# A running sum of squared keys moved from VectorE to GpSimd, with earlier weight cuts, moved stores and re-ordered openings

## The chip, the cores and the metric

The kernel runs on one core of one Trainium2 chip, as one launch. The metric is device time in microseconds (us) of that core. Its engines are TensorE (PE in the profile), VectorE (DVE), ScalarE (ACT), GpSimd (POOL) and SyncE (SP), each with its own instruction stream in program order; they wait for each other by semaphores. DMA queues are fed by the engines that issue the transfers.

## The reference, cut to what matters

Two layers follow each other on x (16 x 128 x 512) with a context ctx of the same shape: first an mLSTM attention over a normalised x and a routed feed-forward layer of eight experts, then cross-attention in 16 heads of 128, with an image part and a text part of the keys, and a feed-forward layer with three-valued weights.

```python
x = x + mlstm(layernorm(x), ctx, ctx)
x = x + routed_ffn(layernorm(x))
x = x + cross_attention(layernorm(x), ctx)
x = x + ternary_linear(x)
# in cross_attention, for the image and the text keys:
k = rms_norm(ctx_part @ k_w + k_b, scale)      # mean of squares over all 16 x 128 columns
q = rms_norm(x @ q_w + q_b, scale)
out = softmax(q k^T / sqrt(128)) v             # per head
```

The change is about the mean of squares in `rms_norm` of the keys: the squares of every head's key rows are added up over the heads, so that one row of sums per token comes out.

## The kernel before

All work is one chain of stages on PE's instruction stream: values (0 to about 195 us), heads (195 to 475), the shared feed-forward part (475 to 560), routed experts (560 to 782), queries (782 to 1005), and attention with the last layer (1005 to the end). float32 products are made as three passes of a leading and a trailing part of each factor (`three_passes`, lines 120 to 122); a weight is therefore cut into a lead (ACT) and a trail (DVE) before PE uses it.

In **heads** two things run interleaved. The mLSTM runs in 4 groups g of 4 batches, with 16 slots n per group, one per head. The keys of the later cross-attention are formed in 64 units u, each 12 matmuls of one head's weight with one group's context; `KEYS` lists them, and a unit stands in a slot of `body(g, first)`. In group 0 the 12 units stand in the slots of `OPENING`, from group 1 on the unit of slot n is u = 16 g + n - 4, and four come after the last slot.

- PE: in each slot a key unit, at n % 4 == 2 scores and outputs, at n % 4 == 3 the turn of the heads (line 1311), which needs hT gathered by DVE (line 1147) in the same slot. A key unit u uses one of three banks and so waits for the square of unit u - 3.
- ACT: the lead of the next unit's weight (`weight_lead`, key_lead, line 1387), exponentials for the decay matrix (line 1008), then key and square of the unit of slot n - 1 (`keep_key`, lines 1045 and 1050). The square waits until the sum of unit u - 2 is done.
- DVE: gather, the decayed matrix of the next slot (line 1120), `weight_trail` (key_trail, line 1392), `add_square` (line 1192, the running sum `total`), and small statistics; in slot 14 it waits for `res_done` and takes the statistics of x_kept (line 137).
- POOL: in each slot the causal mask (line 917) of slot n + 5, and from group 1 on, for the group before, `scale` in slots 8 and 9 (line 935, waits for `fac_done`), `weigh` in 10 and 11 (line 945) and `add` in 12 and 13 (line 954, sends `res_done`). `value` (line 925) runs in slots 5 to 7.
- SP: loads of the slots ahead; in slot 10, after loads that wait for scores, the eight loads of the next group's context parts (of_shared_split from ctx_split, line 1382).

A weight is cut at the unit that first uses it (`FIRST_OF`), into the buffer that alternates by unit. In **values**, SP stores the cut context to ctx_split at u = 30, 32, 34 and 36, beside the stores of the transposed x (line 325) for which ACT waits (line 438). In **routed**, the cuts of the tokens for the second tile (`lead_of`, `trail_of`) stand in the first slot. In **queries**, DVE normalises x in four batches per group and signals once per group; PE then transposes (line 2707).

## Time and profile before

| what | value |
|---|---|
| runs | 1359.07, 1366.83, 1367.22 us; median 1366.83 |
| profiled execution | 1370.19 us, span 1368.5 us |
| mean granted clock of PE | 0.976 |
| busy share of the span | PE 95%, DVE 61%, ACT 54%, POOL 28% |
| heads, 195 to 475 us | PE busy 254.81 of 280.00 us, POOL 131.96, DVE 200.94, ACT 200.73 |

The profile is of one execution, and its times are read from the start of the span. A group of the table of lines has its busy time, the mean of one instruction, and the idle time of the engine before its instructions with what ended it. In the timeline, the bracket at the end of a row is the idle time of the engine before it and the instruction that ended it. Instructions of one engine overlap a little, so the distance between two starts can be shorter than the duration of the first.

### The profile page before, as it was taken

Reading aid. Unit: us, or ns where it says so; the run is one execution under the profiler, and the core shown is the slowest. Engines: PE = TensorE matmul, PEld = TensorE weight load, DVE = VectorE, ACT = ScalarE, POOL = GpSimd, SP = SyncE. Lnnn points to the kernel's source line nnn. Section 1 sums busy time; section 2 is a strip of 40 time slices with the busy share of each in tenths; the row PEclk is TensorE's granted clock in tenths of the full one; section 3 lists DMA queues with packets and bytes.
Section 4 is the critical chain, followed back from the end, with each engine's and each line's share of the span. In section 5 each row is a group of like instructions: output and inputs, shape, how many; then the busy total and the mean of one; then the engine's idle time right before and its main releaser. Section 6 shows DMA issues by size and latency. Waiting matters only on the chain. (4 is left out here: it accounts for less than half of the span.)

```text
span 1368.5 us, 24512 instructions
## 1 busy us (share of the span) xinstructions
PE 1298.8 (95%) x7390; PEld 1072.4 (78%) x7391; DVE 840.9 (61%) x1614; ACT 742.9 (54%) x1839; POOL 382.6 (28%) x358
## 2 busy tenths in 40 slices
PE   7998998989999899899989989999989999999998
PEld 6786876767776768688876678888878888888887
DVE  3644546767679774444444377635477777777865
ACT  4334538786777351345455545544676555556651
POOL 0111014273719006399331153036000000000041
PEclk9999999999999899999999999999999999999999
DMA  7847799877787194675648787473565555555403
GB/s 250 307 186 266 265 319 311 267 252 244 258 254 231 63 333 183 204 218 156 201 147 269 265 256 214 137 232 132 185 202 161 162 158 165 159 168 155 122 32 123
DMA packets 168183, 280.99 MB, mean 205 GB/s; under 512 B 29920, under 2 KB 58336, under 8 KB 167840
## 3 DMA queue, kind: packets, MB, share of 16 engines
q1 hardware_dynamic: 142288, 224.44, 51.6%
q0 software_dynamic: 8672, 29.37, 6.6%
q10 hardware_dynamic: 17136, 26.09, 5.2%
q8 instruction: 47, 0.77, 0.2%
q14 instruction: 40, 0.33, 0.1%
HBM read 171.04 MB, written 108.80 MB: 204 GB/s over the span
## 5 line engine op out<-in xcount | busy, mean ns | idle before, releaser
L120 PE MATMUL banks<-of_shared_split,key_lead 128*128 128x512 f32 x256 | 110.0, 430 | 17.5 <-DVE key_trail L1392 10.7
L2973 ACT ACTIVATE prob<-banks,attend_row,rq 128x128 f32<-128x128 f32 x248 | 110.4, 470 | 0.0
L2986 ACT ACTIVATE attend_ol<-banks,of_attend_vbias 128x512 fp32r<-128x512 f32 x64 | 44.2, 691 | 116.9 <-PE banks L3185 116.9
L120 PE MATMUL banks<-wo,attend_ol 128*128 (+1 forms) x256 | 106.3, 415 | 0.0
L121 PE MATMUL banks<-of_shared_split,key_lead 128*128 128x512 f32 x256 | 104.9, 410 | 0.0
L122 PE MATMUL banks<-of_shared_split,key_trail 128*128 128x512 f32 x256 | 104.8, 410 | 0.0
L120 PE MATMUL banks<-queries_rows_split,queries_wl 128*128 128x512 f32 x256 | 100.9, 394 | 0.0
L122 PE MATMUL banks<-wo,attend_ot 128*128 (+1 forms) x256 | 100.8, 394 | 0.0
L121 PE MATMUL banks<-wo,attend_ol 128*128 (+1 forms) x256 | 100.0, 391 | 0.0
L122 PE MATMUL banks<-queries_rows_split,queries_wt 128*128 128x512 f32 x256 | 99.9, 390 | 0.0
L121 PE MATMUL banks<-queries_rows_split,queries_wl 128*128 128x512 f32 x256 | 99.8, 390 | 0.0
L2955 POOL TENSOR_TENSOR x_kept<-x_kept,attend_tern_bias 128x512 f32<-128x512 f32 x12 | 15.5, 1293 | 282.9 <-ACT of_attend_raw L3012 281.0
L2623 DVE TENSOR_TENSOR queries_total<-queries_total,queries_sq 128x512 f32<-128x512 f32 x60 | 45.5, 759 | 74.8 <-ACT queries_sq L2536 74.8
L2532 ACT ACTIVATE queries_head<-banks,queries_bias 128x512 f32<-128x512 f32 x64 | 44.1, 689 | 81.7 <-PE banks L122 76.5
L1008 ACT ACTIVATE heads_dec<-mlstm_gmax,mlstm_nat 128x128 f32<-128x128 f32 x264 | 83.7, 388 | 8.5 <-POOL mlstm_gmax L917 4.8
L120 PE MATMUL banks<-of_shared_split,of_ctx_lead 128*128 128x512 f32 x208 | 84.3, 406 | 1.4 <-DVE of_ctx_trail L479 1.2
L1192 DVE TENSOR_TENSOR heads_total<-heads_total,heads_ksq 128x512 f32<-128x512 f32 x60 | 54.8, 913 | 45.2 <-ACT heads_ksq L1050 45.2
L122 PE MATMUL banks<-of_shared_split,of_ctx_trail 128*128 128x512 f32 x208 | 82.1, 395 | 0.0
L121 PE MATMUL banks<-of_shared_split,of_ctx_lead 128*128 128x512 f32 x208 | 82.0, 394 | 0.0
L3074 DVE TENSOR_TENSOR x_kept<-x_kept,banks 128x512 f32 (+1 forms) x64 | 44.0, 688 | 60.8 <-PE banks L122 60.2
L120 PEld LDWEIGHTS banks<-of_shared_split,key_lead 128*128 128x128 f32 x256 | 51.0, 199 | 35.6 <-DVE key_trail L1392 14.5
L917 POOL TENSOR_SCALAR_AFFINE_SELECT mlstm_gmax<-mlstm_gmax 128x512 f32<-128x512 f32 x69 | 52.6, 777 | 78.6 <-DMA mlstm_gmax<-running_max 78.4
(399 smaller groups left out, 3569.5 us busy)
## 6 DMA issues: line engine op xcount, KB each, us to landing
mlstm_gmax<-running_max SPq DMA_DIRECT2D x36, 512.0 KB, 5.8
k_heads<-heads_key ACTq DMA_DIRECT2D x64, 256.0 KB, 4.5
q_heads<-queries_head SPq DMA_DIRECT2D x64, 256.0 KB, 2.7
q_ahead<-q_heads SPq DMA_DIRECT2D x64, 256.0 KB, 4.2
of_attend_k<-k_heads SPq DMA_DIRECT2D x60, 256.0 KB, 4.0
of_attend_v<-v_heads SPq DMA_DIRECT2D x60, 256.0 KB, 3.3
key_raw<-in_L_xattn_ki_w SPq DMA_DIRECT2D x20, 512.0 KB, 5.4
sorted_rows<-of_shared_split SPq DMA_DIRECT2D x2, 5120.0 KB, 28.6
```

The source lines that it names most:

```text
L120: nc.tensor.matmul(out, lead_l, lead_r, start=first, stop=False)
L121: nc.tensor.matmul(out, lead_l, trail_r, start=False, stop=False)
L122: return nc.tensor.matmul(out, trail_l, lead_r, start=False, stop=last)
L917: nc.gpsimd.affine_select(out=t, in_=t, compare_op=ALU.is_ge, fill=FAR, base=0, pattern=[[0, GB], [1, S]], channel_multiplier=-1).then_inc ...
L1008: ins = nc.scalar.activation(dec[:, n % 2, b], gmax[:, h // 2 % 4, h % 2 * N + b * S:h % 2 * N + (b + 1) * S], ACT.Exp, scale=-1.0, bias=M ...
L1192: nc.vector.tensor_tensor(t, t, ksq[:, m % 2, :], ALU.add).then_inc(total_done, 1)
L2532: nc.scalar.activation(head[:, u % HEADS_RING, :], ps[:, u % 4, :], ACT.Identity, bias=bias[:, h:h + 1]).then_inc(head_done, 1)
L2623: nc.vector.tensor_tensor(t, t, sq[:, u % 2, :], ALU.add).then_inc(total_done, 1)
L2955: nc.gpsimd.tensor_tensor(K.x[:, b, :], K.x[:, b, :], tern_bias[:], ALU.add).then_inc(tern_bias_done, 1)
L2973: ins = nc.scalar.activation(prob[:, j % 2, b, :], ps[:, j % 2, b * S:(b + 1) * S], ACT.Exp, bias=row[:, j % 2, 1, b:b + 1], scale=rq[:, b ...
L2986: nc.scalar.activation(ol[:, par, j, :], ps[:, 4 + j % 2, :], ACT.Identity, bias=vbias[:, bass.ds(quad_of(it) * 4 + j, 1)]).then_inc(ol_do ...
L3074: nc.vector.tensor_tensor(xb, xb, ps[:, 6 + b % 2, :], ALU.add).then_inc(acc_done, 1)
```

## The change

The running sum of squares moves from DVE to POOL, for all units but the last five, which stay on DVE in the tail. In POOL's body it stands behind the mask and ahead of `value`, `scale`, `weigh` and `add`. The order of `KEYS` changes so that in the middle pairs the two units with the same weight stand next to each other; weight buffers alternate by weight; lead and trail of a weight are formed in the slot `SPLIT_AT`, up to one unit ahead of its first use. The split loads of slot 10 come first in that slot. In the tail the last units' operations are re-ordered on ACT and DVE. In values the stores to ctx_split go out at u = 21, 22, 25 and 26, and a load of x one unit later. In routed the cuts of the second tile come before other cuts. In queries the normalised batches are signalled one by one, and for the first group PE transposes batch by batch.

```diff
-        TOKENS = {4: 0, 5: 1, 7: 2, 9: 3}
+        TOKENS = {4: 0, 5: 1, 8: 2, 9: 3}
+        SPLITS = {21: 0, 22: 1, 25: 2, 26: 3}
...
-                if u % 2 == 0 and 30 <= u < 30 + 2 * G:
-                    g = (u - 30) // 2
+                if u in SPLITS:
+                    g = SPLITS[u]
...
-            for k in range(G + 1) for p in range(HALF // 2) for g in (k - 1, k) if 0 <= g < G for j in range(2)]
+            for k in range(G + 1) for p in range(HALF // 2)
+            for g, j in ([(g, j) for g in (k - 1, k) for j in range(2)] if p in (0, HALF // 2 - 1) else
+                         [(g, j) for j in range(2) for g in (k - 1, k)]) if 0 <= g < G]
...
+    SPLIT_AT = [0, 0] + [max(LAST_OF[v - 2] + 2, FIRST_OF[v] - 1) for v in range(2, VISITS)]
+    FORMED = dict((SPLIT_AT[v], v) for v in range(2, VISITS))
...
                 for n in range(PER):
+                    if not first and not last and n == PER - 2 - LAG:
+                        sp.wait_ge(product, CLOSES[g - 1] + 1)
+                        for part in range(2 * C):
+                            A.load_split(sp, g + 1, part)
...
-                    if not first and not last and n == PER - 2 - LAG:
-                        sp.wait_ge(product, CLOSES[g - 1] + 1)
-                        for part in range(2 * C):
-                            A.load_split(sp, g + 1, part)
...
+            def add_square(g, m):
+                u = unit_number(g, m)
+                of = KEYS[u][1]
+                t = total[:, of * N:(of + 1) * N]
+                pool.wait_ge(ksq_done, u + 1)
+                if u == OPENS[of]:
+                    nc.gpsimd.tensor_scalar(t, ksq[:, m % 2, :], 1.0, None, ALU.mult).then_inc(total_done, 1)
+                else:
+                    pool.wait_ge(total_done, u)
+                    nc.gpsimd.tensor_tensor(t, t, ksq[:, m % 2, :], ALU.add).then_inc(total_done, 1)
+
             def body(g, first):
                 for n in range(PER):
                     mask(g, n + AHEAD)
+                    keys_at(g, n, -1, add_square, first)
...
-                if u == FIRST_OF[v] and v >= 2:
+                if u in FORMED:
+                    v = FORMED[u]
                     act.wait_ge(product, LAST_OF[v - 2] + 1)
-                    A.weight_lead(act, KEYS[u][0], v // 4)
+                    A.weight_lead(act, KEYS[FIRST_OF[v]][0], v // 4)
...
                     keys_at(g, n, 1, weight_trail, first)
-                    keys_at(g, n, -1, add_square, first)
...
+            finish(PER - LAG)
             quad(last, QUADS - 1)
             divisor(last)
+            finish(PER - LAG + 1)
             close(last, 0)
             close(last, 1)
-            finish(PER - LAG)
-            finish(PER - LAG + 1)
+            weight_trail(last, PER - LAG + 3)
...
+            lead_of((0, 1))
+            cut_gate_up(1)
+            slots(act, slot)
+            store_hidden(move(LAST, -2))
+            hidden_lead((0, 0))
+            hidden_lead((0, 1))
+            keep_hidden(move(LAST, -1))
...
-                    ins = nc.vector.tensor_scalar(stage[:, g % 2, b, :], K.x[:, at, :], K.mv[:, at, 0:1],
-                                                  K.rstd[:, at:at + 1], ALU.subtract, ALU.mult)
-                ins.then_inc(staged, 1)
+                    nc.vector.tensor_scalar(stage[:, g % 2, b, :], K.x[:, at, :], K.mv[:, at, 0:1],
+                                            K.rstd[:, at:at + 1], ALU.subtract, ALU.mult).then_inc(staged, 1)
...
-            for t in range(C):
-                turn(t)
+            for b in range(GB):
+                pe.wait_ge(staged, b + 1)
+                for c in range(C):
+                    ins = nc.tensor.transpose(ps[:, bank(c), b * S:(b + 1) * S], stage[:, 0, b, c * P:(c + 1) * P], K.ident[:])
+                    if b == GB - 1:
+                        ins.then_inc(turned, 1)
```

On POOL, slots 9 to 13 of group 1 stood like this before (the mask of a slot, then two operations for the group before; heads_sq is its scaled heads, x_kept the residual):

```order
L917 AFFINE_SELECT mlstm_gmax<-mlstm_gmax 128x512
L935 TENSOR_TENSOR heads_sq<-heads_hraw,heads_small 128x512 x2
L917 AFFINE_SELECT mlstm_gmax<-mlstm_gmax 128x512
L945 TENSOR_TENSOR heads_sq<-heads_sq,heads_lnb 128x512 x2
L917 AFFINE_SELECT mlstm_gmax<-mlstm_gmax 128x512
L945 TENSOR_TENSOR heads_sq<-heads_sq,heads_lnb 128x512 x2
```

Now an addition stands in each slot between the mask and the two operations (L973 is the new `add_square`; the lines of the others have moved by 6):

```order
L923 AFFINE_SELECT mlstm_gmax<-mlstm_gmax 128x512
L973 TENSOR_TENSOR heads_total<-heads_total,heads_ksq 128x512
L941 TENSOR_TENSOR heads_sq<-heads_hraw,heads_small 128x512 x2
L923 AFFINE_SELECT mlstm_gmax<-mlstm_gmax 128x512
L973 TENSOR_TENSOR heads_total<-heads_total,heads_ksq 128x512
L951 TENSOR_TENSOR heads_sq<-heads_sq,heads_lnb 128x512 x2
L923 AFFINE_SELECT mlstm_gmax<-mlstm_gmax 128x512
L973 TENSOR_TENSOR heads_total<-heads_total,heads_ksq 128x512
L951 TENSOR_TENSOR heads_sq<-heads_sq,heads_lnb 128x512 x2
```

So each of these slots has three two-input operations in place of two, and the first waits for ACT's square of the slot before.

On SP, the loads around slot 10 of group 1 stood like this (mlstm_gmax, mlstm_q and mlstm_kT are for slots ahead, of_shared_split is the next group's context):

```order
L819 DMA mlstm_gmax<-running_max 128x1024
L813 DMA mlstm_q<-xn_turned 128x512
L816 DMA mlstm_kT<-ctx_turned 128x512
L1382 DMA of_shared_split<-ctx_split 128x512 x8
L819 DMA mlstm_gmax<-running_max 128x1024
```

Now the eight split loads come ahead of the slot's other three:

```order
L1402 DMA of_shared_split<-ctx_split 128x512 x8
L825 DMA mlstm_gmax<-running_max 128x1024
L819 DMA mlstm_q<-xn_turned 128x512
L822 DMA mlstm_kT<-ctx_turned 128x512
L825 DMA mlstm_gmax<-running_max 128x1024
```

Here the eight loads moved past one load of mlstm_gmax and the pair of mlstm_q and mlstm_kT.

## Rows read from the trace of the kernel before

**Rows 1.** The page: busy time of each engine, share of the span, instructions.

```profile
PE 1298.8 (95%) x7390; PEld 1072.4 (78%) x7391; DVE 840.9 (61%) x1614; ACT 742.9 (54%) x1839; POOL 382.6 (28%) x358
```

**Rows 2.** Waits of PE: line, waited for, us in total, times, longest.

```profile
PE banks L120 <- DVE key_trail L1392: 10.7, 9, 4.0
...
PE banks L120 <- DMA of_shared_split<-ctx_split: 6.8, 3, 3.8
PE banks L120 <- DVE routed_ht L2189: 4.8, 2, 2.5
```

**Rows 3.** Windows: stretch, length; busy PE, PEld, DVE, ACT, POOL; clock, DMA share, GB/s.

```profile
306.50:313.30 6.80, 6.00 (x21) 4.43 (x24) 1.89 (x3) 1.74 (x3) 1.22 (x2) 0.50 0.94 352
...
120.00:130.00 10.00, 9.07 (x49) 7.34 (x48) 2.50 (x4) 4.01 (x7) 5.86 (x4) 1.00 1.05 408
```

**Rows 4.** Timeline of PE in heads: start, duration, engine, line, operation, wait before it.

```profile
282.62 0.40 PE L122 MATMUL banks<-of_shared_split,key_trail 128*128 128x512 f32 x1
...
307.30 0.80 PE L120 MATMUL banks<-of_shared_split,key_lead 128*128 128x512 f32 x1 [3.84 <-DMA of_shared_split<-ctx_split]
...
318.30 0.48 PE L120 MATMUL banks<-of_shared_split,key_lead 128*128 128x512 f32 x1
...
347.15 0.40 PE L122 MATMUL banks<-of_shared_split,key_trail 128*128 128x512 f32 x1
...
380.60 0.48 PE L120 MATMUL banks<-of_shared_split,key_lead 128*128 128x512 f32 x1
...
408.38 0.40 PE L122 MATMUL banks<-of_shared_split,key_trail 128*128 128x512 f32 x1
...
440.00 0.48 PE L120 MATMUL banks<-of_shared_split,key_lead 128*128 128x512 f32 x1
```

**Rows 5.** Groups of lines: busy us, mean ns of one, idle time before them.

```profile
L1192 DVE TENSOR_TENSOR heads_total<-heads_total,heads_ksq 128x512 f32<-128x512 f32 x60 | 54.8, 913 | 45.2 <-ACT heads_ksq L1050 45.2
L954 POOL TENSOR_TENSOR x_kept<-x_kept,heads_sq 128x512 f32<-128x512 f32 x12 | 19.0, 1600 | 0.0
L917 POOL TENSOR_SCALAR_AFFINE_SELECT mlstm_gmax<-mlstm_gmax 128x512 f32<-128x512 f32 x69 | 52.6, 777 | 78.6 <-DMA mlstm_gmax<-running_max 78.4
```

**Rows 6.** Timeline of POOL in slots 8 to 13 of group 1.

```profile
283.60 2.52 POOL L935 TENSOR_TENSOR heads_sq<-heads_hraw,heads_small 128x512 f32<-128x512 f32 x2 [4.54 <-DVE heads_small L1175]
...
286.68 2.51 POOL L935 TENSOR_TENSOR heads_sq<-heads_hraw,heads_small 128x512 f32<-128x512 f32 x2
...
292.68 1.09 POOL L917 TENSOR_SCALAR_AFFINE_SELECT mlstm_gmax<-mlstm_gmax 128x512 f32<-128x512 f32 x1
...
301.84 2.97 POOL L954 TENSOR_TENSOR x_kept<-x_kept,heads_sq 128x512 f32<-128x512 f32 x2
```

**Rows 7.** Timeline of DVE in slots 14 and 15 of group 1.

```profile
309.09 1.28 DVE L137 BATCH_NORM_STATS2 stats<-x_kept 128x6 f32<-128x512 f32 x2
...
315.21 0.69 DVE L1147 COPY heads_hT<-banks 128x512 f32<-128x512 f32 x1 [4.84 <-PE banks L1304]
...
316.42 0.68 DVE L1392 TENSOR_TENSOR key_trail<-key_raw,key_lead 128x512 fp32r<-128x512 f32 x1
```

**Rows 8.** Timeline of ACT: the squares of slot 7's unit, groups 1 and 3.

```profile
286.76 0.67 ACT L1050 ACTIVATE heads_ksq<-banks,heads_kbias 128x512 f32<-128x512 f32 x1
...
414.18 0.67 ACT L1050 ACTIVATE heads_ksq<-banks,heads_kbias 128x512 f32<-128x512 f32 x1
```

**Rows 9.** Timeline of DVE in the tail of heads: the last addition.

```profile
461.14 0.69 DVE L1192 TENSOR_TENSOR heads_total<-heads_total,heads_ksq 128x512 f32<-128x512 f32 x1
```

**Rows 10.** Timelines of ACT and PE in values.

```profile
131.19 0.60 ACT L438 ACTIVATE mlstm_gmax<-banks 128x512 f32<-128x512 f32 x1 [4.90 <-DMA xn_turned<-mlstm_gmax]
...
132.32 0.78 PE L649 MATMUL banks<-x_lead,values_w_x 128*128 128x512 f32 x1 [3.25 <-ACT x_lead L441]
```

**Rows 11.** Timelines of DVE and PE at the opening of queries.

```profile
800.62 0.59 DVE L2605 TENSOR_SCALAR of_attend_raw<-x_kept,mv,rstd 128x512 f32<-128x512 f32 x1
...
802.70 0.69 PE L2707 MATMUL banks<-ident,of_attend_raw 128*128 128x128 f32 x2 [3.74 <-DVE of_attend_raw L2605]
```

More of the change, by code:

```diff
@@ L293, in _ @@
                 if u in TOKENS:
-                    if u > 4:
+                    if u % 4:
                         sp.wait_ge(product, u - 1)
                     load_x(TOKENS[u])
-                if u % 2 == 0 and 30 <= u < 30 + 2 * G:
-                    g = (u - 30) // 2
+                if u in SPLITS:
+                    g = SPLITS[u]
                     sp.wait_ge(trail_done, (g + 1) * C)
@@ L719, in heads_and_keys @@
     LAST_OF = [max(u for u, key in enumerate(KEYS) if key[2] == v) for v in range(VISITS)]
+    SPLIT_AT = [0, 0] + [max(LAST_OF[v - 2] + 2, FIRST_OF[v] - 1) for v in range(2, VISITS)]
+    FORMED = dict((SPLIT_AT[v], v) for v in range(2, VISITS))
+    assert len(FORMED) == VISITS - 2
     OPENS = [min(u for u, key in enumerate(KEYS) if key[1] == g) for g in range(G)]
@@ L827, in next_raw @@
                 u = unit_number(g, m)
-                v = KEYS[u][2]
-                if u == FIRST_OF[v] and v % 2 and v // 2 + 2 < VISITS // 2:
+                v = FORMED[u] if u in FORMED else u if u < 2 else 0
+                if v % 2 and v // 2 + 2 < VISITS // 2:
                     sp.wait_ge(wt_done, v + 1)
@@ L1030, in weight_lead @@
                 u = unit_number(g, m)
-                v = KEYS[u][2]
-                if u == FIRST_OF[v] and v >= 2:
+                if u in FORMED:
+                    v = FORMED[u]
                     act.wait_ge(product, LAST_OF[v - 2] + 1)
-                    A.weight_lead(act, KEYS[u][0], v // 4)
+                    A.weight_lead(act, KEYS[FIRST_OF[v]][0], v // 4)
             def keep_key(g, m):
@@ L1074, in _ @@
             last = G - 1
-            row_sums(last)
             for m in range(PER - LAG, PER + 1):
-                if m + 1 < PER:
+                if m < PER - LAG + 2:
                     weight_lead(last, m + 1)
                 keep_key(last, m - 1)
+                if m == PER - LAG:
+                    row_sums(last)
                 if m == PER - LAG + 1:
+                    weight_lead(last, m + 2)
                     square(last, 0)
@@ L1178, in weight_trail @@
                 u = unit_number(g, m)
-                v = KEYS[u][2]
-                if v >= 2 and u == FIRST_OF[v]:
-                    A.weight_trail(dve, v, KEYS[u][0])
+                if u in FORMED:
+                    v = FORMED[u]
+                    A.weight_trail(dve, v, KEYS[FIRST_OF[v]][0])
             def add_square(g, m):
@@ L1248, in _ @@
             variance(last, 0)
-            finish(PER - LAG + 2)
+            add_square(last, PER - LAG + 1)
             variance(last, 1)
@@ L1323, in keys @@
                 for c in range(C):
-                    ins = three_passes(nc, ps[:, KEY_BANKS[u % 3], :], wl[:, m % 2, c, :], wt[:, m % 2, c, :], part(0, c),
+                    ins = three_passes(nc, ps[:, KEY_BANKS[u % 3], :], wl[:, v % 2, c, :], wt[:, v % 2, c, :], part(0, c),
                                        part(1, c), c == 0, c == C - 1)
@@ L2094, in slot @@
             def slot(t):
-                if counts(t, 1):
+                if counts(t, 2):
                     lead_of(t)
@@ L2104, in slot @@
                     silu(move(t, -1))
-            act.wait_ge(raw_loaded[0], 32)
-            cut_piece(0)
-            lead_of((0, 0))
-            for c in range(1, C):
-                cut_piece(c)
-            cut_gate_up(1)
-            slots(act, slot)
-            store_hidden(move(LAST, -2))
-            keep_hidden(move(LAST, -1))
-            silu(LAST)
-            store_hidden(move(LAST, -1))
             def hidden_lead(t):
@@ L2124, in hidden_lead @@
                                      ).then_inc(hl_done, 1)
+            act.wait_ge(raw_loaded[0], 32)
+            cut_piece(0)
+            lead_of((0, 0))
+            for c in range(1, C):
+                cut_piece(c)
+            lead_of((0, 1))
[5 more added lines that the diff above has]
+            keep_hidden(move(LAST, -1))
+            silu(LAST)
+            store_hidden(move(LAST, -1))
             def keep(t):
@@ L2140, in second_slot @@
                     store_hidden(LAST)
-            second_slot((0, 0))
-            second_slot((0, 1))
             act.wait_ge(gu, TILES)
@@ L2193, in slot @@
             def slot(t):
-                if counts(t, 1):
+                if counts(t, 2):
                     trail_of(t)
@@ L2205, in _ @@
                 cut_piece(c)
+            trail_of((0, 1))
             cut_gate_up(1)
             slots(dve, slot)
-            hidden(LAST)
             hidden_trail((0, 0))
             hidden_trail((0, 1))
+            hidden(LAST)
             for e in range(4, E):
@@ L2477, in _ @@
                                             ALU.mult).then_inc(wl_done, 1)
-            pool.wait_ge(staged, G)
+            pool.wait_ge(staged, G * GB)
             pool.wait_ge(small_loaded, 16 * sum(late == 0 for *_, late in A.loads))
@@ L2702, in turn @@
                 g, c = divmod(t, C)
-                pe.wait_ge(staged, g + 1)
+                pe.wait_ge(staged, (g + 1) * GB)
                 if t >= C:
```

## The prediction

> **What bounds the kernel now.** I read the page's busy times first: TensorE is busy in 95% of the span and no other engine in more than 61% [rows 1]. So time can only be won where PE waits, or where its clock is low. The table of PE's waits came next [rows 2]: in heads PE waits 6.8 us for the ctx_split transfers and, over the whole program, 10.7 us for key_trail on DVE. The windows show the second price of a wait: from 306.5 to 313.3 us, around the 3.84 us wait before 307.30, the granted clock is 0.50, which is 1.2 GHz instead of 2.4 [rows 3, 4]. 6.8 us at half clock do the work of 3.4 us, so a wait of this size costs its own length and up to 3.4 us more. The reader is to keep three questions apart: how long PE waits, what clock it has after that, and which engine ends the wait.
>
> **The running sum on POOL.** Per group of heads, 16 additions of 128x512 leave DVE (60 in all, 913 ns each [rows 5], of which the last five stay) and come to POOL. DVE was not the bound, so what it saves is worth little by itself. POOL has work that is waited for: in slots 8 to 13 of groups 1, 2 and 3 it scales, weighs and adds the group before (12 two-input operations), and DVE waits in slot 14 for the last of them (res_done) before it takes the statistics, gathers hT and so lets PE turn the heads. Before, this chain went from 283.60 to 304.81 us (301.84 + 2.97), and DVE came to its end only at 309.09 [rows 6, 7]: 4.3 us of slack, nobody waits.
>
> After, POOL's order in each slot is mask, addition, then the old operations. The chain cannot begin before the square of slot 7's unit, since that addition stands ahead of the first scale. Call t7 the end of PE's unit in slot 7: 283.02, 347.55 and 408.78 in the three groups (the starts of their last matmuls plus 0.40 [rows 4]). ACT's square of that unit ends at 286.76 + 0.67 = 287.43, so 4.4 us after t7 in group 1; I take the same in group 2; in group 3 it ends at 414.85, 6.1 us after [rows 8]. From there POOL has 6 additions, 12 old operations and 5 masks. A two-input operation starts 1.25 us after the one before it (2.52 for two), a mask takes about 0.61 (283.60 + 2.52 to 286.68 [rows 6]): 18 x 1.25 + 5 x 0.61 = 25.6 us. Three or four key_trail operations on DVE fall into it; beside one a mask took 1.09 [rows 6], so some 0.45 more each, 1.6 us. The chain is 27.2 us and ends at t7 + 31.6 (group 3: 33.3).
>
> Behind it on DVE stand two statistics (1.28), the gather and the decayed row (1.21 from the gather's start to the trail's) and key_trail (0.68) [rows 7]. All but the last few tenths are on the path to the next unit, which starts at t7 + 31.6 + 1.28 + 0.65 + 1.2 = t7 + 34.8 (group 3: 36.9 with its 6.1 and 0.2 more for the trail). Before, the unit behind each group's slot 15 started at 318.30, 380.60 and 440.00 [rows 4], which is t7 + 35.3, + 33.05 and + 31.2. So the three groups change by -0.5, +1.75 and +5.7: +7.0 us. The ctx_split waits (3.84 and 2.74 us) and the half clock that follows are inside the old 35.3 and 33.05; they go, because the split loads are now issued ahead of a load that waited for scores, and the new wait eats what they give.
>
> Without waits PE would be ready for the turn at about t7 + 27.9, 28.4 and 29.2 in the three groups (the old 35.3 - 3.84 - 3.4, 33.05 - 2.74 - 1.7 and 31.2 less some 1.8 of short waits, each less 0.2 for the turn), and gets hT at 33.55 (group 3: 35.2), so it waits 5 to 6 us each time. After such waits the clock was 0.50 for 6.8 us [rows 3]; I book 3.4 us for groups 1 and 2 and none in group 3, whose last units wait for DVE anyhow: +6.8. The bounds are 0 (clock kept) and 10.2.
>
> The Trainium skill, "GPSIMD Engine Reference", section 4.1, gives VectorE for an elementwise addition, with GpSimd about 2x slower on two inputs; this speaks against the change. The trace agrees in the direction: 1.25 us against an undisturbed 0.69 on DVE [rows 6, 9], a factor of 1.8. By the page's factor an operation would be 1.38, the chain 2.3 us longer, and the whole 7 us slower than the sum below.
>
> **Weights cut a unit earlier.** Lead and trail of most weights move one unit ahead and alternate by visit. PE's waits for key_trail come to 10.7 us in nine places [rows 2]. The longest, 4.0, lies in the tail; of the other 6.7 in eight I take 2.7 as won, the four that lie in slots 4 to 7 of groups 1 and 2, where a weight is now cut a unit earlier. The tail goes from 440.00 to the last addition at 461.14 + 0.69 [rows 4, 9]; there DVE sets the end, and with the re-ordered finish I count 1.4 us less, the two additions of 0.69 that no longer stand between.
>
> Heads together: 7.0 + 6.8 - 2.7 - 1.4 = +9.7 us.
>
> **The moved stores in values.** ACT waits 4.90 us for the store of mlstm_gmax into xn_turned, then PE 3.25 us for x_lead at 132.32 [rows 10]. That store is in the same queues as the ctx_split stores, when DMA is full (120 to 130: share 1.05, 408 GB/s [rows 3]). The change sends these stores at units 21 to 26, some 30 us earlier. I take the wait of 3.25 as gone; its half clock and two units slowed beside it give 0.5 to 3.4 more, I take 0.6: -3.8. Zero is the other bound, if the late store is late by itself.
>
> **Openings of routed and queries.** In routed the lead and trail of the second tile come earlier, but behind 579.99 the next weight's cut waits for a raw load that lands only at about that time, and at 719 DVE's hidden product stands behind other cuts; of the waits there (4.8 us for routed_ht alone [rows 2]) I count 0.9. In queries PE waits 3.74 us before 802.70 for all four normalised batches [rows 11]; each now has its own signal, so the first transposes can start 1.5 us earlier (three of the four operations of 0.59, which overlap to about 0.5 each [rows 11]), and with the shorter half clock I count 3.0. Bounds: 0 and 3.74 + 3.4.
>
> **Sum.** +9.7 - 3.8 - 0.9 - 3.0 = +2.0 us. The profiled execution took 1370.19, which would become 1372.2; it lies 3.4 above the median of the runs shown, 1366.83, so the forecast for the median is 1369.
>
> **Rivals.**
> A. The chain on POOL does not reach PE. Then the next units start at PE's own pace, t7 + 28.1, 28.6 and 29.3: -7.2, -4.4 and -1.9, with no new half clock; with -4.1 from the weights heads wins some 17.5, the other stages 7.7, together -25: 1342. It needs a chain 5 us shorter, so additions that cost nearly nothing between the old operations. Against it stands that 6 x 1.25 and a start 3.8 us later are 11 us, and the slack was 4.3.
> B. The other side: additions are dearer, because POOL and DVE hinder each other. With the mean of the adds in x_kept, 1.600, for all 18 and the masks' mean 0.777 [rows 5] the chain is 28.8 + 3.9 = 32.7, 5.5 more in each of three groups: +16.5, 1385. It passes 1% slower at 3.8 us more per group, which is a mean of about 1.5 us per operation. For it speaks that those means were taken in this stretch; against it that DVE loses its own additions there (0.91 each [rows 5]), so that less runs beside POOL. The Trainium skill, "SBUF — State Buffer", section "Who interferes with whom", has a DVE operation with two SBUF inputs and a GpSimd operation that reads SBUF exclude each other for the whole instruction. By that each of four key_trails would cost 0.68 in place of 0.45, 1 us per group, 1372; the 0.45 of the row is less than a whole instruction.
> C. The openings and stores give nothing (the waits move on): +7.7, 1377.
> D. The chain delays PE, but the clock stays up: -6.8, 1362.
>
> **How the numbers follow.** The sum with its neighbours C and D holds 0.64 of the chance, A 0.16, B 0.20. About 1%, 13.7 us, is what a measurement of this kernel can tell from no change: faster by more (under 1353) is A, 0.17 with the lower edge of D; slower by more (over 1380.5) is B, 0.19; within 1% 0.64. The range leaves out most of A and the worst of B: 1350 to 1387. The likeliest case by itself, with the unknown clock and openings, is 1362 to 1377.
>
> **What would show it.** Right: in slots 14 and 15 of groups 1 to 3 PE waits 4 to 7 us for the turn's hT, behind statistics on DVE that wait for x_kept on POOL; ctx_split is gone from PE's waits; POOL's operations there follow each other without gaps at about 1.25 us; half clock stands behind the first two of these waits. Wrong, towards A: DVE reaches the statistics after POOL's last add. Towards B: operations of 1.5 us and more in the chain and waits of 10 us. The prediction fails altogether if POOL's additions delay ACT's squares so far that PE waits for a bank in every slot; the trace gives no such sign, since a unit needs only the square of the third unit before it.

## The result and the profile after

The changed kernel takes 1372.4 us (median of 8 runs, 1370.14 to 1376.81), the kernel before 1366.4 in the same comparison: a ratio of 1.0046, interval 1.0024 to 1.0068. So it is half a per cent slower, which is within the 1% that was forecast as "same", 3.4 us above the 1369 of the prediction and inside its range.

Where PE and DVE wait shows the mechanism at once. From the tables of waits of the changed kernel, of PE (first four rows) and of DVE (the last): engine, line, waited for, us in total, times, longest us.

```profile
PE banks L1331 <- DVE heads_hT L1167: 13.7, 4, 5.2
PE banks L120 <- DVE key_trail L1412: 12.0, 11, 2.4
...
PE banks L1368 <- DVE heads_total L1212: 3.3, 1, 3.3
...
PE banks L120 <- DMA of_shared_split<-ctx_split: 1.2, 1, 1.2
...
DVE stats L137 <- POOL x_kept L960: 27.7, 3, 9.8
```

The wait for the ctx_split transfers, 6.8 us before [rows 2], is down to 1.2. In its place PE waits 13.7 us for hT, and DVE, which was never late for res_done before [rows 7], waits three times, up to 9.8 us, for POOL's last addition into x_kept. The waits for key_trail, 10.7 before, have not gone but grown to 12.0.

The chain on POOL in slots 8 to 14 of group 1 answers to [rows 6]; L973 is the new addition. Columns as there.

```profile
284.14 1.30 POOL L973 TENSOR_TENSOR heads_total<-heads_total,heads_ksq 128x512 f32<-128x512 f32 x1 [1.71 <-ACT heads_ksq L1068]
285.39 2.06 POOL L941 TENSOR_TENSOR heads_sq<-heads_hraw,heads_small 128x512 f32<-128x512 f32 x2
287.41 0.64 POOL L923 TENSOR_SCALAR_AFFINE_SELECT mlstm_gmax<-mlstm_gmax 128x512 f32<-128x512 f32 x1
288.01 1.28 POOL L973 TENSOR_TENSOR heads_total<-heads_total,heads_ksq 128x512 f32<-128x512 f32 x1
...
305.79 1.30 POOL L973 TENSOR_TENSOR heads_total<-heads_total,heads_ksq 128x512 f32<-128x512 f32 x1
307.05 2.50 POOL L960 TENSOR_TENSOR x_kept<-x_kept,heads_sq 128x512 f32<-128x512 f32 x2
```

It begins when ACT's square is there, runs without a gap and ends at 309.55. What stands behind it on DVE, and PE at the turn (first matmul of the turn and of the next unit, in groups 1, 2 and 3):

```profile
309.59 1.29 DVE L137 BATCH_NORM_STATS2 stats<-x_kept 128x6 f32<-128x512 f32 x2 [9.84 <-POOL x_kept L960]
310.79 0.67 DVE L1167 COPY heads_hT<-banks 128x512 f32<-128x512 f32 x1
311.38 0.68 DVE L1140 SCALAR_TENSOR_TENSOR heads_cmat<-banks,heads_dec 128x512 f32<-128x512 f32 x1
311.98 1.11 DVE L1412 TENSOR_TENSOR key_trail<-key_raw,key_lead 128x512 fp32r<-128x512 f32 x1
```

```profile
311.52 0.66 PE L1331 MATMUL banks<-ident,heads_hT 128*128 128x128 f32 x4 [3.85 <-DVE heads_hT L1167]
313.15 0.80 PE L120 MATMUL banks<-of_shared_split,key_lead 128*128 128x512 f32 x1 [0.97 <-DVE key_trail L1412]
...
374.80 1.11 PE L1331 MATMUL banks<-ident,heads_hT 128*128 128x128 f32 x4 [3.81 <-DVE heads_hT L1167]
376.42 0.79 PE L120 MATMUL banks<-of_shared_split,key_lead 128*128 128x512 f32 x1 [0.51 <-DVE key_trail L1412]
...
440.38 1.12 PE L1331 MATMUL banks<-ident,heads_hT 128*128 128x128 f32 x4 [5.21 <-DVE heads_hT L1167]
442.66 0.79 PE L120 MATMUL banks<-of_shared_split,key_lead 128*128 128x512 f32 x1 [1.16 <-DVE key_trail L1412]
```

DVE ends its wait, takes two statistics, then gathers; PE waits 3.8, 3.8 and 5.2 us for that, and about 1 us more for the trail. Beside each of the three waits the granted clock falls to 0.50, the lower of its two levels (1.2 GHz in place of 2.4), for 3.4, 6.8 and 6.8 us. The windows over these stretches, columns as in [rows 3]:

```profile
312.90:316.30 3.40, 3.15 (x7) 2.48 (x8) 3.40 (x6) 2.97 (x8) 2.74 (x4) 0.50 0.55 210
...
374.30:381.10 6.80, 5.79 (x15) 4.43 (x16) 6.09 (x9) 3.71 (x10) 5.31 (x6) 0.50 0.30 109
...
439.20:446.00 6.80, 4.45 (x12) 3.38 (x13) 6.80 (x9) 0.69 (x1) 6.80 (x6) 0.50 0.59 198
```

Outside heads, the wait of 3.25 us of [rows 10] is gone (the same matmul starts with no wait in front), and the 3.74 us of [rows 11] are 1.53:

```profile
131.89 0.48 PE L650 MATMUL banks<-x_lead,values_w_x 128*128 128x512 f32 x1
...
804.89 1.30 PE L2747 MATMUL banks<-ident,of_attend_raw 128*128 128x128 f32 x9 [1.53 <-DVE of_attend_raw L2627]
```

### The profile page after: what moved, and what is told of

It reads as the page before. It is cut to its first block and busy times, and to the rows that moved or that the text cites. A ratio compares the mean times of both kernels' runs of the same rounds, so it can differ in the third digit from the quotient of the medians.

```text
span 1368.5 us, 24513 instructions
## 1 busy us (share of the span) xinstructions
PE 1293.2 (94%) x7390; PEld 1069.8 (78%) x7391; DVE 814.4 (60%) x1555; ACT 743.6 (54%) x1839; POOL 444.6 (32%) x417
## 5 line engine op out<-in xcount | busy, mean ns | idle before, releaser
L120 PE MATMUL banks<-of_shared_split,key_lead 128*128 128x512 f32 x256 | 107.9, 422 | 13.2 <-DVE key_trail L1412 12.0
L121 PE MATMUL banks<-of_shared_split,key_lead 128*128 128x512 f32 x256 | 103.4, 404 | 0.0
L973 POOL TENSOR_TENSOR heads_total<-heads_total,heads_ksq 128x512 f32<-128x512 f32 x55 | 72.2, 1313 | 56.2 <-ACT heads_ksq L1068 56.2
L122 PE MATMUL banks<-of_shared_split,of_ctx_trail 128*128 128x512 f32 x208 | 82.8, 398 | 0.0
L120 PEld LDWEIGHTS banks<-of_shared_split,key_lead 128*128 128x128 f32 x256 | 50.1, 196 | 30.6 <-DVE key_trail L1412 16.1
L3191 PEld LDWEIGHTS banks<-attend_kn,q_ahead 128*128 128x128 f32 x496 | 66.1, 195 | 6.2 <-issue 1.9
## 6 DMA issues: line engine op xcount, KB each, us to landing
sorted_rows<-of_shared_split SPq DMA_DIRECT2D x2, 5120.0 KB, 28.3
```

The source lines that it names most:

```text
L120: nc.tensor.matmul(out, lead_l, lead_r, start=first, stop=False)
L121: nc.tensor.matmul(out, lead_l, trail_r, start=False, stop=False)
L122: return nc.tensor.matmul(out, trail_l, lead_r, start=False, stop=last)
L973: nc.gpsimd.tensor_tensor(t, t, ksq[:, m % 2, :], ALU.add).then_inc(total_done, 1)
L3191: ins = nc.tensor.matmul(ps[:, j % 2, s], q[:, j, s], kn[:, j % 2, s], start=True, stop=True)
```

## The experiments

Each kernel was timed against the kernel before on the same chip. The runs fall into four such comparisons, in which the median of the kernel before lay between 1366.4 and 1368.8 us, so kernels are to be compared by their ratios. The theory under test: POOL's addition stands in the chain that ends in res_done, DVE stands behind that wait with hT, and PE behind DVE. Rival 1: the additions are harmless where they stand, but POOL's reads slow DVE. Rival 2: the loss comes from the new order of weights and tail.

| run | what | ratio to before | interval | median us |
|---|---|---|---|---|
| (the change) | all of it | 1.0046 | 1.0024 to 1.0068 | 1372.4 |
| e1 | change, sum back on VectorE | 0.9941 | 0.9915 to 0.9966 | 1360.5 |
| e2 | before, only the sum on GpSimd | 1.0057 | 1.0035 to 1.0078 | 1376.1 |
| e3 | change, statistics behind the turn | 0.9983 | 0.9963 to 1.0004 | 1366.7 |
| e4 | change, addition last in POOL's slot | 0.9961 | 0.9935 to 0.9987 | 1364.2 |
| e5 | before, only values, routed, queries | 0.9954 | 0.9930 to 0.9979 | 1361.0 |
| e6 | before, only the weights | 0.9974 | 0.9953 to 0.9995 | 1365.4 |
| e7 | e1 with the old tail | 0.9896 | 0.9860 to 0.9932 | 1352.8 |
| e8 | change, sum on VectorE in 6 slots | 0.9945 | 0.9919 to 0.9972 | 1360.0 |
| e9 | e7, in the tail a trail first and the last addition earlier | 0.9875 | 0.9843 to 0.9906 | 1351.5 |
| e10 | change with the old tail | 1.0033 | 1.0008 to 1.0057 | 1372.9 |
| e11 | before, only the split loads | 0.9931 | 0.9910 to 0.9952 | 1359.4 |

**e1: the sum alone undone.**

```diff
 # POOL, body
-                    keys_at(g, n, -1, add_square, first)
 # DVE, body, behind weight_trail
+                    keys_at(g, n, -1, add_square, first)
```

> The changed kernel with the running sum back on VectorE; all else of the change stays. Theory (the chain on POOL ends the wait in slots 14 and 15): the next unit behind slot 15 comes back from 34 to about 29 us after the end of slot 7's unit in three groups, and the half clock behind these waits goes: 15 to 20 us less than the changed kernel, 1353 to 1357 us, 0.989 to 0.993 of the kernel before. Rival 1 (the sum itself is harmless; POOL's reads slow DVE's key_trail from 0.81 to 1.06 us and PE waits for those): 2 to 4 us less, 1368 to 1370 us. Rival 2 (what heads loses comes from the order of weights and the tail): no change, 1372 us, heads still 9 us longer than before.

Measured: 0.9941; between the two ratios lie 1.05%, some 14 us. Of PE's 13.7 us of waits for hT 1.7 are left, none over 0.8. The next units start 30.6, 29.1 and 31.3 us after the end of slot 7's unit; in the change it is 33.9, 33.9 and 36.2. The longest wait in heads is now the one before the sums, which was 3.3 us:

```profile
PE banks L120 <- DVE key_trail L1412: 13.5, 13, 3.2
...
PE banks L1368 <- DVE heads_total L1211: 6.0, 1, 6.0
```

The theory holds in place and kind; of its 15 to 20 us 14 were measured. Rival 1 (2 to 4 us) and rival 2 (none) fall. What was not foreseen is the 6.0 us before the sums, which e7 takes up.

**e2: the sum alone, on the kernel before.**

```diff
 # POOL, body, behind mask
+                    keys_at(g, n, -1, add_square, first)
 # DVE, body
-                    keys_at(g, n, -1, add_square, first)
```

> The kernel before with nothing changed but the running sum on POOL, in the place it has in the changed kernel. Theory: the next unit behind slot 15 comes 34 to 36 us after the end of slot 7's unit in groups 1 to 3, against 35.3, 33.05 and 31.2 before, and the key_trail waits stay: 5 to 12 us more than the kernel before, 1371 to 1378 us, 1.004 to 1.009. Rival 1 (contention): 1 to 3 us more and no wait for hT in slot 15. Rival 2 (order of weights and tail): no change, 1366 us.

Measured: 1.0057, 7.8 us more. In groups 1 and 2 PE is held by the split loads, as before (4.4 and 3.5 us, before 3.8 and 2.7), and the chain is hidden behind that; in group 3, which has no split loads, it waits 5.3 us for hT:

```profile
PE banks L120 <- DMA of_shared_split<-ctx_split: 7.9, 2, 4.4
...
PE banks L1322 <- DVE heads_hT L1159: 6.1, 2, 5.3
```

The sum on POOL costs by itself, and the two waits lie over one another: where PE waits for the split loads, the chain costs little more. The traces show the other side of this too. Moving the split loads alone (e11) brings the next unit of groups 1 and 2 nearer to the end of slot 7's unit by 4.3 and 4.4 us (35.3 and 33.1 before, 31.0 and 28.6 in e11); with the sum on POOL it is 1.1 us each (35.0 in e2, 33.9 in the change, which differ in other edits as well).

**e3: the same work on POOL, but nobody waits for it.**

```diff
-                        if n >= PER - GB // 2:
-                            if n == PER - GB // 2:
-                                dve.wait_ge(res_done, FIRST + g)
-                            for b in range(2):
-                                row_stats.batch((g - 1) * GB + 2 * (n - PER + GB // 2) + b)
+                        if n == PER - 1:
+                            dve.wait_ge(res_done, FIRST + g)
+                            for b in range(GB):
+                                row_stats.batch((g - 1) * GB + b)
```

> The changed kernel; DVE waits for res_done, and takes all four statistics, only behind the gather, the decayed row and key_trail of slot 15, so hT no longer waits for POOL. POOL's work and its order stay. Theory: PE turns the heads at its own time, the waits of 4 to 5 us for hT go, DVE is late by 2 to 4 us in the next group's slot 0, of which PE sees 0 to 3: 8 to 15 us less than the changed kernel, 1357 to 1364 us, 0.993 to 0.998. Rival 1 (contention): nothing gained, 1372 us, since POOL and DVE read at the same times as before. Rival 2: no change.

Measured: 0.9983, 0.6% or 8.6 us less than the change, at the lower edge of the theory, with every addition still on POOL. So it is the wait and what is queued behind it that costs. What is left has other causes. In slot 15 of group 1 PE waits for a trail, which waits for its lead on ACT, which is queued behind an earlier key. ACT, then DVE, then PE at the next unit:

```profile
298.38 0.34 ACTq L1072 DMA_DIRECT2D k_heads<-heads_key  x1
...
307.67 0.69 ACT L1063 ACTIVATE heads_key<-banks,heads_kbias 128x512 f32<-128x512 f32 x1 [4.59 <-issue]
...
308.92 0.63 ACT L1406 ACTIVATE key_lead<-key_raw 128x512 fp32r<-128x512 f32 x1
```

```profile
309.58 1.65 DVE L1411 TENSOR_TENSOR key_trail<-key_raw,key_lead 128x512 fp32r<-128x512 f32 x1 [2.28 <-ACT key_lead L1406]
```

```profile
311.28 0.50 PE L120 MATMUL banks<-of_shared_split,key_lead 128*128 128x512 f32 x1 [1.95 <-DVE key_trail L1411]
```

The key operation of 307.67 writes one of two key buffers and needs the store that was issued from it at 298.38; in the trace that store lands at 307.58, 0.1 us before the key starts. So this wait of 4.59 us is one for a store and not for POOL, and the kernel before has it too (2.9 and 3.3 us, in groups 1 and 2). POOL does reach PE in a second way, since ACT's square of a unit waits until the sum of the second unit before it is done (`total_done`), but only in group 3: there three squares wait 1.0 to 2.5 us and start 0.1 us behind the end of a sum. The tail became longer: from its first unit to the sums are 28.3 us, in the change 23.2. DVE now has all four statistics right ahead of its tail work; no run shows how much of the 5.2 us is theirs.

**e4: the addition last in POOL's slot.**

```diff
                     mask(g, n + AHEAD)
-                    keys_at(g, n, -1, add_square, first)
...
                                 step(g - 1, 2 * (n - at) + 1)
+                    keys_at(g, n, -1, add_square, first)
```

> The changed kernel; in POOL's slot the addition stands behind value, scale, weigh and add in place of ahead of them. The same operations run. Theory: the chain begins with a scale 1.7 us earlier and its last addition stands behind res_done, so res_done comes about 3.3 us earlier in three groups and PE's wait there falls from 4 to 5 us to 1 to 2: 9 to 13 us less with the clock, 1359 to 1363 us, 0.995 to 0.998. Rival 1 (contention): no change, 1372 us. Rival 2: no change, 1372 us.

Measured: 0.9961, 0.85% or 11.6 us less than the change, as expected. The same operations, and PE's wait for hT is a third:

```profile
PE banks L1331 <- DVE heads_hT L1167: 4.8, 4, 2.0
```

In this trace the stretch ahead of the first chain, from the first key unit to the end of slot 7 of group 1, is 6.8 us longer than in the change (89.6 and 82.8); how much of that comes with the edit no run shows.

**e5: the parts outside heads alone** (the diffs of values, routed and queries as in the change).

> The kernel before with the edits of values, routed and queries alone; heads is untouched. Theory (these openings give what the stages of the changed kernel's trace show: heads starts 3.1 us earlier, routed to its down products 2.7, from there to the first query unit 3.7): 8 to 10 us less than the kernel before, 0.993 to 0.994. Rival (the waits move on, or are of that one execution): 0 to 3 us less, 0.998 to 1.000.

Measured: 0.9954, 6.3 us less; the interval is 2.9 to 9.6, which holds the predicted 7.7 and does not separate it from the 9.5 that the stages of one execution show (3.1 + 2.7 + 3.7).

**e6: the weights alone** (the new order of `KEYS`, `SPLIT_AT`, buffers by weight).

> The kernel before with the new order of KEYS and the weights formed at SPLIT_AT alone; sum, split loads and tail as before. Theory (as predicted): the waits for key_trail in slots 4 to 7 of groups 1 and 2 go, 2 to 4 us less, 0.997 to 0.999. Rival: the order does harm, since leads and trails now come at other slots in which ACT and DVE are late: 2 us more or worse, 1.002.

Measured: 0.9974, 3.6 us less, beside the predicted 2.7; the harm that the rival asks for isn't there. The waits for key_trail in slots 4 to 7 of groups 1 and 2 are gone, two of 0.8 us; others came, and PE's total is 10.2 us in place of 10.7. So the rows of waits do not show where the 3.6 us come from.

**e7 and e10: the old tail**, with the sum on VectorE (e7) and on GpSimd (e10). The edit of both on DVE, against e1 and against the change; on ACT the leads of the tail and the row sums go back to their old places as well:

```diff
 # DVE, tail of heads
-            finish(PER - LAG)
             quad(last, QUADS - 1)
             divisor(last)
-            finish(PER - LAG + 1)
             close(last, 0)
             close(last, 1)
-            weight_trail(last, PER - LAG + 3)
+            finish(PER - LAG)
+            finish(PER - LAG + 1)
...
-            add_square(last, PER - LAG + 1)
+            finish(PER - LAG + 2)
```

> The changed kernel with the sum back on VectorE, as in the first run, and besides the tail of heads in its old order on ACT and DVE. Theory: in the new tail the trail and the addition ahead of the last quad push DVE's serial chain to the last addition 2 to 3 us back, and PE's sums wait 6.0 us for it; with the old tail the stretch from the first tail unit to the sums falls from 23.5 to about 20.5 and a little half clock goes: 3 to 5 us less than the first run, 0.990 to 0.992 of the kernel before. Rival (as predicted: the new order of the tail gains 1.4): 1 to 2 us more than the first run, 0.995.

> The changed kernel, sum on GpSimd, with the tail of heads alone in its old order on ACT and DVE. Theory: what the prediction missed lies in the tail, booked at 1.4 us less but in truth 4 to 7 us more: 4 to 7 us less than the changed kernel, 0.999 to 1.002 of the kernel before, with the waits for hT in slot 15 still there. Rival (with the sum on POOL the tail's order does not matter, since DVE is late by the wait in slot 14 anyway): as the changed kernel, 1.004.

Measured: e7 0.9896, e10 1.0033. With the sum on VectorE PE's wait before the sums falls from e1's 6.04 to 1.09:

```profile
446.89 4.00 PE L1354 MATMUL banks<-ones,heads_total 128*128 128x1 f32 x32 [1.09 <-DVE heads_total L1198]
```

From the first tail unit (425.90) to the sums are 21.0 us, in e1 23.5 (426.56 to 450.05). In ratios e7 is 0.45% below e1, but the two were compared with the kernel before at different times and their intervals overlap a little; 2.5 us of it is what the traces show in this stretch, and 3.6 in the next, from the sums to the first matmul of the shared part (18.7 us in e1, where the clock is at 0.50 for 13.7 us, and 15.0 in e7, where it is so for 3.4). In e10 the theory is not borne out: 1.0033 against 1.0046 can't be told apart, and from the first tail unit to the sums are 22.7 us, in the change 23.2. There the tail starts behind a wait of 5.2 for hT in either order.

**e8: the sum on VectorE in slots 8 to 13 of groups 1 to 3 only.**

```diff
 # POOL, body
-                    keys_at(g, n, -1, add_square, first)
+                    if first or not 8 <= n < 14:
+                        keys_at(g, n, -1, add_square, first)
 # DVE, body, behind weight_trail
+                    if not first and 8 <= n < 14:
+                        keys_at(g, n, -1, add_square, first)
```

> The changed kernel; in slots 8 to 13 of groups 1 to 3 alone (18 of 55 additions) the sum is added on VectorE, in all other slots on GpSimd. Theory (only the additions inside the chain of the old twelve operations matter): as the first run, in which all are on VectorE, within 3 us: 0.992 to 0.996 of the kernel before, no wait for hT in slot 15. Rival (POOL's additions are dear wherever they stand, by contention with DVE's trails or by the way from engine to engine): 1366 us or more, 0.999 or more.

Measured: 0.9945, e1 has 0.9941. In the total the 37 additions still on POOL cost nothing that can be measured (the two intervals leave some 5 us open); the 18 of the chain cost all of it. Nor do the 37 bring anything that can be measured, as VectorE was not the bound. Place by place it is not nothing: in slot 2 of groups 2 and 3 PE waits 2.7 and 3.4 us for heads_cmat, each time with 6.8 us at the clock of 0.50, where e1's longest such wait anywhere is 1.1. DVE and PE in group 2:

```profile
315.77 1.19 DVE L1148 TENSOR_TENSOR heads_small<-heads_small,mlstm_nat 128x64 f32<-128x64 f32 x1 [3.88 <-ACT heads_small L1034]
```

```profile
320.07 2.09 PE L1315 MATMUL banks<-mlstm_q,mlstm_kT 32*128 32x128 f32 x32 [2.71 <-DVE heads_cmat L1141]
```

The small operation on DVE takes 1.19 us beside an addition on POOL and 0.22 in e1, where DVE adds. From the start of the next unit to the end of the following slot 7 it is 33.0 and 33.3 us, in e1 28.9 and 28.8; ahead of the first chain, in the tail and up to the shared part e8's trace is shorter.

**e9: trail first, addition later, in the tail.**

```diff
 # DVE (against e7; ACT's lead goes with it)
+            weight_trail(last, PER - LAG + 1)
             quad(last, QUADS - 1)
...
-            finish(PER - LAG)
+            add_square(last, PER - LAG - 1)
 # the last addition
+                if b == 1:
+                    finish(PER)
             own(ins)
-            finish(PER)
```

> The seventh run's kernel (sum on VectorE, old tail) with two things moved in the tail: lead and trail of the second tail unit's weight come ahead of the last quad (the addition stays behind it), and the last addition comes behind two of the four scaling products in place of behind all four. Theory (in the tail a trail ahead of the quad helps PE and an addition there hurts the chain): PE's wait of 4.0 us for key_trail at the second tail unit goes, the sums come 2 to 4 us earlier: 0.986 to 0.988 of the kernel before. Rival (DVE's serial chain sets the end of heads whatever stands ahead): as the seventh run, 0.989 to 0.991.

Measured: 0.9875, 1351.5 us; that of e7, 0.9896, lies within its interval. It is 1.2% faster than the kernel before and 1.7% faster than the changed one, but what it adds to e7 is not shown by the times. In the traces the sums come 2.0 us earlier after the first tail unit (19.0 us, in e7 21.0), the least that the theory asks for. The wait for the trail is only shifted, from 3.99 at the second tail unit to 2.75 at the third.

```profile
436.00 0.50 PE L120 MATMUL banks<-of_shared_split,key_lead 128*128 128x512 f32 x1 [2.75 <-DVE key_trail L1401]
```

**e11: the split loads alone.**

```diff
                 for n in range(PER):
+                    if not first and not last and n == PER - 2 - LAG:
+                        sp.wait_ge(product, CLOSES[g - 1] + 1)
+                        for part in range(2 * C):
+                            A.load_split(sp, g + 1, part)
...
-                    if not first and not last and n == PER - 2 - LAG:
-                        sp.wait_ge(product, CLOSES[g - 1] + 1)
-                        for part in range(2 * C):
-                            A.load_split(sp, g + 1, part)
```

> The kernel before with the eight split loads of slot 10 moved ahead of that slot's other loads, and nothing else. Theory (the gain that the chain on POOL ate): PE's waits for ctx_split of 6.8 us in slots 14 and the half clock behind them go: 6 to 10 us less, 0.993 to 0.996. Rival (the split loads are held by something else, so the wait moves to another load or to slot 15): 0 to 2 us less, 0.999.

Measured: 0.9931, 9.4 us less. No wait for ctx_split stands in the table of PE's waits any more, and the unit that waited 3.84 us [rows 4] goes on. Of the parts that were timed alone this move is the largest gain (e5 has 6.3 us and e6 3.6; the intervals of e5 and e11 overlap), and in the changed kernel it was hardly to be seen, since the chain on POOL took its place.

## Why the prediction was right

**The chain** is what it said: additions, scale, weigh and add without a gap from ACT's square to res_done. Predicted 27.2 us, measured 25.4 in groups 1 and 2 and 26.3 in group 3; its end was to be t7 + 31.6 (33.3), it was 30.3, 30.3 and 31.9. Of the 1.8 us too many in groups 1 and 2, 0.9 are in the scaling, booked at 1.25 each from [rows 6], of which two take 2.06 here. The 2.52 us for two in those rows held a trail or an addition on DVE, and the change takes the additions away: a row of before was read as the price of the operation alone. The rest was hindrance by key_trail, of which less came than booked (two POOL operations of 0.45 more in group 1, in place of 1.6 us).

**The next unit** was to start at t7 + 34.8, 34.8 and 36.9 (the parts that are named add up to 34.7 and 36.7). The last matmuls of slot 7's units start at

```profile
278.81 0.40 PE L122 MATMUL banks<-of_shared_split,key_trail 128*128 128x512 f32 x1
...
342.14 0.40 PE L122 MATMUL banks<-of_shared_split,key_trail 128*128 128x512 f32 x1
...
406.11 0.40 PE L122 MATMUL banks<-of_shared_split,key_trail 128*128 128x512 f32 x1
```

so the units at 313.15, 376.42 and 442.66 are at t7 + 33.9, 33.9 and 36.2: 0.7 to 0.9 us earlier each. The three groups change by -1.3, +0.8 and +4.9, +4.4 in all; the prediction had +7.0. PE waited 3.8, 3.8 and 5.2 us for hT where "5 to 6" stood: it was ready for the turn at t7 + 28.5, about as estimated, and hT came 1.3 us sooner.

**Clock and weights between the groups.** +6.8 for new half clock and -2.7 for the trails, +4.1 together. From the start of the next unit to the end of the following slot 7 the two stretches took 29.25 and 28.18 us before (318.30 to 347.55, 380.60 to 408.78 [rows 4]) and take 29.39 and 30.09 now: +2.1. Half clock did stand behind the first two waits, but for 3.4 us behind the first, where 6.8 were booked; it stood behind the third as well, where none was booked. The trails are where the working was thin. The prediction counts four waits, 2.7 us, in slots 4 to 7 of groups 1 and 2; the trace of before has two there, 0.78 and 0.79. Those did go, as e6 shows by itself, but three of 0.6 to 0.8 came up in slot 9 and three of 0.5 to 1.2 at the next unit.

**The tail** is the term that failed: -1.4 was booked, for two additions "that no longer stand between". In truth a trail and an addition went ahead of the last quad, in front of the chain that ends in the last addition. From the first tail unit to the sums are 23.2 us (442.66 to 465.82), before 21.9 (440.00 to 461.88): +1.3. Behind it the clock stays low longer, 1.6 us more from the sums to the first matmul of the shared part (16.7 and 18.2); but e5, e6 and e11, whose tails are as before, have the same 18.2, so this is not the tail's. By e1 and e7 PE's wait before the sums is one for DVE's chain in its new order. By e10 the order is not what cost in the changed kernel itself: the prediction worked the tail out apart from the wait for hT, and behind that wait DVE comes late into the tail from slot 14 in either order.

**Heads together** was to be +9.7 us; from the first key unit to the first matmul of the shared part it is +8.6 in the profiled executions (279.0 to 287.6). That is nearer than the terms deserve, and luck: against the terms as booked it is -2.6 in the groups, -2.0 between them and -0.7 ahead of the first chain, and on the other side +2.7 in the tail and +1.6 behind it.

**Outside heads** -7.7 was booked. By stages of the two executions values gives 3.1 (3.8 booked), and routed and the opening of queries give 6.3 (3.9 booked), while the shared part itself is 0.8 longer; timed alone, e5, the edits give 6.3 with an interval that holds both.

**The sum** was +2.0 on the profiled execution. The profiled executions took 1370.19 and 1370.25, no change; the medians differ by 6 us. The step that missed is thus the last: the offset of 3.4 us between the profiled execution of before and its median was carried over to the changed kernel, whose profiled execution lies 2.2 below its median. A median from three runs was a thin base as well: in the four comparisons the median of before is 1366.4 to 1368.8. That the forecast still lies 3.4 us from the measured median owes something to luck, since the terms err by more than that one by one. A term in us from one execution is no better than a few us for this kernel, whose runs spread over 7 to 14.

**The rivals.** A, chain hidden, has its place in e1 and e8: 1360, not 1342. The new tail took part of the difference; with the old one (e7) it is 1352.8, and where the rest is was not tested. B, dear additions, did not come: POOL's addition has a mean of 1.31 us, not 1.6:

```profile
L973 POOL TENSOR_TENSOR heads_total<-heads_total,heads_ksq 128x512 f32<-128x512 f32 x55 | 72.2, 1313 | 56.2 <-ACT heads_ksq L1068 56.2
L1412 DVE TENSOR_TENSOR key_trail<-key_raw,key_lead 128x512 fp32r<-128x512 f32 x40 | 42.5, 1064 | 7.7 <-ACT key_lead L1407 7.5
```

C fell with e5, and D with the window at 0.50 above.

The factor of 2 that the Trainium skill, "GPSIMD Engine Reference", section 4.1, gives for a two-input operation is near what the rows show (1.28 for an undisturbed addition on POOL, 0.69 on DVE). Its advice, VectorE for elementwise work, is borne out in the slots of the chain (e1, e8) and makes no difference to the total in the others (e8).

## What to carry to other kernels

Before work is moved to an idle engine, look for the chain on that engine that somebody waits for, and put the new operations behind it or outside it: here the 18 additions cost 14 us inside the chain; behind each slot's old work (e4) the loss is 2 to 3 us, which is within the noise, and in the other slots nothing shows in the total (e8). A wait in one engine's stream holds everything queued behind it: e3 gave back 8.6 us by moving the wait alone behind work that PE needs. When several edits are made at once, time each alone: one edit worth 9 us was hidden by another, and it needed none of the rest. Nor do such gains add up: e5, e6 and e11 alone come to 19 us, and together with the old tail (e7) they gave 14, though the intervals leave some 5 us open.

A row of the kernel before also holds the hindrance of the work that the change takes away. The scaling was booked at 1.25 us and took 1.05, because DVE's additions were no longer there.

## What was not expected of the hardware

DVE and POOL do not both become slower where they meet: one of them waits for the other's whole operation. POOL, then DVE, in the changed kernel:

```profile
440.80 1.26 POOL L973 TENSOR_TENSOR heads_total<-heads_total,heads_ksq 128x512 f32<-128x512 f32 x1
```

```profile
440.85 1.76 DVE L1412 TENSOR_TENSOR key_trail<-key_raw,key_lead 128x512 fp32r<-128x512 f32 x1
```

The trail, 0.68 us alone, begins 0.05 us after the addition and ends 0.55 us after it. Of the 40 trails of this kernel 17 begin while a two-input operation runs on POOL, and each of the 17 ends 0.55 or 0.56 us after that operation; the 11 beside which POOL stands idle take 0.68 or 0.69. So what a trail loses is what is left of the POOL operation: up to 1.1 us.

The other way round an operation on POOL takes 0.45 us more when a two-input operation of DVE was already waiting as it began. The scaling in the kernel before and in the changed one (least, median and longest in ns):

```profile
L935 POOL TENSOR_TENSOR heads_sq<-heads_hraw,heads_small x12: 1044/1273/1516, 283.6 to 415.8; 128x512 f32<-128x512 f32 x12
...
L941 POOL TENSOR_TENSOR heads_sq<-heads_hraw,heads_small x12: 1042/1049/1056, 285.4 to 418.3; 128x512 f32<-128x512 f32 x12
```

Before, six of the twelve take 1.05 us, and the six with a trail or an addition of DVE waiting take 1.50 to 1.52; in the changed kernel none has one. The additions into x_kept go the same way, 1.28 free and mostly 1.73 behind DVE, so that their mean falls from 1.60 to 1.27 as DVE's additions leave. By the Trainium skill, "SBUF — State Buffer", section "Who interferes with whom", a DVE operation with two SBUF inputs contends with a GpSimd operation that reads SBUF, and the lock is exclusive; these rows agree with that.
